# A recurrence in fp32 products, and its two halves with banks, semaphores and tanh of their own

## The reference, cut to what matters

```python
xb = jnp.einsum('bsd,ed->sbe', x, B)

def step(h, xb_t):
    h = jnp.tanh(h @ A.T + xb_t)
    y = h @ C.T
    return (h, y)
```

## Time and profile before

| | us |
|---|---|
| median of 3 runs | 909.51 |
| lowest and highest | 907.95, 910.41 |
| the profiled execution | 910.45 |
| its span, first to last instruction | 908.6 |
| the recurrence in it, from the first tanh to the first product with C | 36.40 to 83.57 |

### The profile page before, as it was taken

How to read it: one execution, slowest core, us unless ns; L and a number is a source line. 1 busy time by engine, 2 the same in 40 slices (tenths; PEclk the granted TensorE clock), 3 DMA queues, 4 the chain that set the end, 5 groups by cost and what they waited for, 6 DMA issues and landing times.

```text
span 908.6 us, 13681 instructions
## 1 busy us (share of the span) xinstructions
PE 785.4 (86%) x4875; PEld 599.0 (66%) x4954; DVE 349.3 (38%) x1002; ACT 250.1 (28%) x583; POOL 133.2 (15%) x100
## 2 busy tenths in 40 slices
PE   8878779999972668897896989999998988999997
PEld 5466439988541334564574558999984555999995
DVE  1434650000319996545765742111114551111113
ACT  1222114433243340436166122212220021122221
POOL 1000020000204991012204030000004012000004
PEclk9855889999995999799997979999999979999998
DMA  9500056995132532000000044999954024799972
GB/s 338 219 3 2 1 223 223 323 306 196 32 107 61 152 99 105 1 0 1 0 1 0 1 161 151 321 319 321 323 208 156 0 71 191 231 327 320 320 235 84
DMA packets 39590, 139.27 MB, mean 153 GB/s; under 512 B 5744, under 2 KB 20288, under 8 KB 27904
## 3 DMA queue, kind: packets, MB, share of 16 engines
q1 hardware_dynamic: 37312, 132.88, 43.4%
q0 software_dynamic: 2240, 5.90, 1.9%
HBM read 127.40 MB, written 11.35 MB: 153 GB/s over the span
## 4 chain that ended last, share of the span: by engine, by line
PE 66%; DVE 14%; DMA 5%; issue 5%; ACT 5%; POOL 3%; DVEq 0%; POOLq 0%; SPq 0%; ACTq 0%
PE PS L428 63%; DVE arena L1616 4%; POOL arena L1216 2%; DMA arena<-x_slots 1%; DVE stats L1297 1%; PE PS L485 1%; PE PS L451 1%; POOL arena L1229 1%; DMA arena<-y_slots,posu 1%; DMA arena<-w_moe 1%; ACT arena L1012 1%; DMA x_slots<-XH,posu 1%; ACT XT L911 1%; DMA y_slots<-arena 1%; DMA arena<-bc_scratch 0%
## 5 line engine op out<-in xcount | busy, mean ns | idle before, releaser
L428 PE MATMUL PS<-arena 128*128 128x128 f32 (+4 forms) x3348 | 421.6, 280 | 28.1 <-ACT arena L1012 9.8
L428 PEld LDWEIGHTS PS<-arena 128*128 128x128 f32 (+2 forms) x3348 | 368.7, 172 | 69.5 <-issue 18.3
L428 PE MATMUL PS<-warm 128*128 128x512 bf16 (+1 forms) x397 | 106.4, 379 | 14.8 <-DVE rs L1281 9.0
L1441 DVE TENSOR_TENSOR arena<-arena,PS 128x384 f32<-128x384 f32 (+1 forms) x62 | 30.3, 488 | 199.2 <-ACT arena L949 199.2
L428 PEld LDWEIGHTS PS<-warm 128*128 128x128 bf16 x476 | 46.4, 100 | 66.9 <-DVE rs L1281 12.9
L1216 POOL DMA_INDIRECT arena<-y_slots,posu x25 | 23.9, 954 | 384.6 <-DMA y_slots<-arena 377.9
L949 ACT ACTIVATE arena<-PS 128x384 f32<-128x384 f32 x62 | 30.4, 490 | 162.2 <-PE PS L428 162.2
L428 PE MATMUL PS<-arena,ident 128*128 128x512 f32 (+1 forms) x128 | 39.6, 456 | 38.1 <-POOL arena L1229 38.1
L1229 POOL TENSOR_TENSOR arena<-arena 128x1152 f32<-128x1152 f32 x16 | 56.1, 3509 | 48.8 <-DVE arena L1616 48.4
L1453 DVE SCALAR_TENSOR_TENSOR H<-arena,wgt,H 128x256 f32<-128x256 f32 (+1 forms) x25 | 11.9, 477 | 124.8 <-DMA arena<-y_slots,posu 124.4
L428 PEld LDWEIGHTS PS<-arena,ident 128*128 128x128 f32 x128 | 21.2, 196 | 56.6 <-POOL arena L1229 40.1
(11 more groups left out here) (253 smaller groups left out, 756.1 us busy)
## 6 DMA issues: line engine op xcount, KB each, us to landing
arena<-w_moe SPq DMA_DIRECT2D x31, 1152.0 KB, 5.7
arena<-w_moe SPq DMA_DIRECT2D x31, 1024.0 KB, 5.2
arena<-w_moe SPq DMA_DIRECT2D x24, 1026.0 KB, 6.6
arena<-bc_scratch SPq DMA_DIRECT2D x32, 288.0 KB, 3.8
arena<-x_slots SPq DMA_DIRECT2D x43, 128.0 KB, 2.2
y_slots<-arena SPq DMA_DIRECT2D x43, 128.0 KB, 5.0
wsh<-w_sh SPq DMA_DIRECT2D x1, 2176.0 KB, 8.3
wl_s<-w_l SPq DMA_DIRECT2D x1, 2048.0 KB
```

The lines of the kernel that those rows point to most:

```text
L428: return nc.tensor.matmul(out_, l, r, start=start, stop=stop, skip_group_check=True)
L1441: ins = v.tensor_tensor(hid_b[x][:, 0:full], sg_s[x][:, 0:full], PS[:, 2 * x + 1, 0:full], ALU.mult)
```

## The change

The three bf16 terms go, of A and of h, with the four splitting instructions of VectorE and its three in every step. A step is now four fp32 products, each a block of the fp32 matrix A (`wrnn_s[:, 0]`) with 16 columns of `HN`, read where tanh wrote them. The two halves of the output have a semaphore each: `rnn_z0` is signalled when half 0 of the sum is complete, `rnn_z1` when half 1 is, and ScalarE does tanh on each half as soon as it is there, one instruction of 16 columns in place of two with 32. TensorE waits for `rnn_h0` before the products that read half 0 of h, and for `rnn_h1` before those that read half 1. Odd and even steps have the four products in different orders.

```diff
--- before.py
+++ after.py
@@ -221,12 +221,6 @@
 
         HN = part(PATCH_K * (T + D), KD, T)
 
-        o_ = PATCH_K * (T + D) + KD * T
-        A_p = part(o_, 3 * KD * D // 2).bitcast(BF16).rearrange("p (i k d) -> p i k d", i=3, k=KD)
-        A_rest = part(o_ + 3 * KD * D // 2, KD, D)
-        h_p = part(o_ + 5 * KD * D // 2, 3 * KD * NB // 2).bitcast(BF16).rearrange("p (i k b l) -> p i k b l", i=3, k=KD, l=1)
-        h_rest = part(o_ + 5 * KD * D // 2 + 3 * KD * NB // 2, KD, NB)
-
         U1 = KD * T
         xs, zs, dr, dl, dx, ys = (part(i * U1, KD, T) for i in range(6))
         dA = [PS[:, 3 + 2 * d:5 + 2 * d, :].rearrange("p b c -> p (b c)")[:, 0:T] for d in range(KD)]
@@ -628,22 +622,28 @@
             last.then_inc(sem("rnn_x"), 1)
             HNv = HN[:, :, :].rearrange("p k (b l) -> p k b l", l=L)
 
-            def rnn_step(lh, at, t):
-
-                for i, (what, parts_of_a) in enumerate((("rnn_h1", 3), ("rnn_h2", 2), ("rnn_h3", 1))):
-                    pe.wait_ge(sem(what), t)
-
-                    for a_ in range(parts_of_a):
-                        for m in range(KD):
-                            for k in range(KD):
-                                last = mm(PS[:, 4 + 2 * lh + m, at:at + NB], A_p[:, a_, k, 128 * m:128 * (m + 1)],
-                                          h_p[:, i, k, :, 0], False, False)
-                return last
-
-            pe.wait_ge(sem("A_split"), 1)
+            def rnn_step(t):
+
+                def product(m, k):
+                    z = PS[:, 4 + 2 * (t % 2) + m, NB * (t // 2):NB * (t // 2 + 1)]
+                    return mm(z, wrnn_s[:, 0, k, 128 * m:128 * (m + 1)], HNv[:, k, :, t - 1], False, False)
+
+                pe.wait_ge(sem("rnn_h0"), t)
+                product(0, 0)
+                if t % 2:
+                    pe.wait_ge(sem("rnn_h1"), t)
+                    product(0, 1).then_inc(sem("rnn_z0"), 1)
+                    product(1, 0)
+                else:
+                    product(1, 0)
+                    pe.wait_ge(sem("rnn_h1"), t)
+                    product(0, 1).then_inc(sem("rnn_z0"), 1)
+                product(1, 1).then_inc(sem("rnn_z1"), 1)
+
             for t in range(1, L):
-                rnn_step(t % 2, NB * (t // 2), t).then_inc(sem("rnn_z"), 1)
-            pe.wait_ge(sem("rnn_h"), L)
+                rnn_step(t)
+            for m in range(KD):
+                pe.wait_ge(sem(f"rnn_h{m}"), L)
             token_products("attn0", lambda k, j: HN[:, k, tsl(j)], KD, lambda k: wrnn_s[:, 2, k, :])
 
 
@@ -1004,13 +1004,12 @@
 
             HNv = HN[:, :, :].rearrange("p k (b l) -> p k b l", l=L)
             act.wait_ge(sem("rnn_x"), 1)
-            nc.scalar.activation(h_p[:, 0], PS[:, 4:6, 0:NB], ACT.Tanh).then_inc(sem("rnn_h1"), 1)
-            nc.scalar.activation(HNv[:, :, :, 0:1], PS[:, 4:6, 0:NB], ACT.Tanh).then_inc(sem("rnn_h"), 1)
-            for t in range(1, L):
-                z = PS[:, 4 + 2 * (t % 2):6 + 2 * (t % 2), NB * (t // 2):NB * (t // 2 + 1)]
-                act.wait_ge(sem("rnn_z"), t)
-                nc.scalar.activation(h_p[:, 0], z, ACT.Tanh).then_inc(sem("rnn_h1"), 1)
-                nc.scalar.activation(HNv[:, :, :, t:t + 1], z, ACT.Tanh).then_inc(sem("rnn_h"), 1)
+            for t in range(L):
+                for m in range(KD):
+                    if t:
+                        act.wait_ge(sem(f"rnn_z{m}"), t)
+                    z = PS[:, 4 + 2 * (t % 2) + m, NB * (t // 2):NB * (t // 2 + 1)]
+                    nc.scalar.activation(HNv[:, m, :, t], z, ACT.Tanh).then_inc(sem(f"rnn_h{m}"), 1)
 
 
             act.wait_ge(sem("lru_reduced"), 1)
@@ -1493,23 +1492,6 @@
                 all_stats(H)
 
 
-            dve.wait_ge(sem("ld_rnn"), 32)
-            link(v.tensor_copy(A_p[:, 0], wrnn_s[:, 0]))
-            link(v.tensor_tensor(A_rest[:, :, :], wrnn_s[:, 0], A_p[:, 0], ALU.subtract))
-            link(v.tensor_copy(A_p[:, 1], A_rest[:, :, :]))
-            v.tensor_tensor(A_p[:, 2], A_rest[:, :, :], A_p[:, 1], ALU.subtract).then_inc(sem("A_split"), 1)
-
-            HNv = HN[:, :, :].rearrange("p k (b l) -> p k b l", l=L)
-            for t in range(L - 1):
-                dve.wait_ge(sem("rnn_h"), t + 1)
-                v.tensor_tensor(h_p[:, 1], HNv[:, :, :, t:t + 1], h_p[:, 0], ALU.subtract).then_inc(sem("rnn_h2"), 1)
-                v.tensor_tensor(h_rest[:, :, :, None], HNv[:, :, :, t:t + 1], h_p[:, 0], ALU.subtract)\
-                    .then_inc(sem("rnn_rest"), 1)
-                dve.wait_ge(sem("rnn_h2"), t + 1)
-                dve.wait_ge(sem("rnn_rest"), t + 1)
-                v.tensor_tensor(h_p[:, 2], h_rest[:, :, :, None], h_p[:, 1], ALU.subtract).then_inc(sem("rnn_h3"), 1)
-
-
             dve.wait_ge(sem("lru_b"), 1)
             c_ = lambda i: lru_c[:, i:i + 1]
             link(v.tensor_scalar(c_(5), c_(2), float(np.pi / 2), None, ALU.add))
```

## The result

| | before | changed |
|---|---|---|
| median of four runs, us | 908.73 | 921.25 |
| lowest and highest, us | 904.72, 910.41 | 919.58, 923.50 |
| the profiled execution, us | 910.45 | 923.50 |
| its span, us | 908.6 | 921.6 |
| first tanh to the first product with C, us | 47.17 | 58.89 |

The ratio of the changed kernel to the one before is 1.0143, with a 95% interval from 1.0113 to 1.0174: 13 us slower, between 10 and 16. The forecast was 923.3, in a range of 916 to 930. One number further down needs a word here: three of the ten executions of e5 ran at a mean clock of 0.90 where the others had 0.94 to 0.95, took 955 to 971 us, and are not in its ratio.

What follows compares the result with a forecast made beforehand. TensorE's weight loads were to bound the recurrence at 1.765 us a step against 1.337 for the three-engine loop; the change costs 13.8 us, taking the profiled 910.45 to 924.3, forecast as 923.3, range 916 to 930.

Steps and rivals of the forecast that it cites:

- The bound: Recurrence: TensorE's own loads replace the three-engine loop as the bound, 1.765 us a step against 1.337.
- A load costs 0.213 us at 1.2 GHz, the columns nothing: Recurrence products: weight loads start 0.213 us apart at the lower clock, and 16 strided columns add nothing to that pace.
- Rival 2: Recurrence: a load costs 107 ns at either clock, so 1.19 us a step and 904.5 us; chance 0.01.
- rival 3: Recurrence: strided columns stand behind each load, 0.266 us per load, 2.13 us a step, 935 us; chance 0.05.
- The clock: Recurrence: TensorE runs at 1.2 GHz after about 38.84 us, as before, with 2.1 steps run until then.
- The way back and the waits: Recurrence: half a result is back 0.76 us after its last load starts; one 0.12 us wait per pair of steps.
- The stage: First tanh to the products with C: these start at 97.4 us instead of 83.57, costing 13.8 us.
- What follows: From the products with C on: the same work later, also beginning at the lower clock, with no cost added.
- VectorE's early start: VectorE's preparation for a later sublayer and first additions to H can run early, but gain nothing.

Runs made afterwards that it cites:

- e5: The changed kernel with three bf16 matmuls of 512 columns added behind every step; ratio 0.9999 to the kernel before.
- e3: The changed kernel with 64 in place of 128 stationary columns in each product of the recurrence; 898.51 us, ratio 0.9874 to the kernel before.
- e6: The kernel before with its bf16 terms, each half of the channels given its own semaphore, tanh and splitting instructions; ratio 1.0014.
- e10: The changed kernel itself run again beside the kernel before on the same chip; 925.41 us, ratio 1.0143.
- e7: The kernel before with two bf16 matmuls of 512 columns added per step; ratio 0.9945.
- e9: The kernel before with two bf16 matmuls of 512 columns added per step, run once more; ratio 0.9951.

## Why the prediction was right

- **The bound.** Right: TensorE's loads stand in a row in place of the way round three engines. VectorE has nothing to do in the window (0.00 us busy).
- **A load costs 0.213 us at 1.2 GHz, the columns nothing.** Right, shown by e3 (0.107 for half the width) and by 0.213 from start to start in the stretch (0.216 with the waits). Rival 2 (107 ns at either clock) and rival 3 (columns behind the load) fall.
- **The clock.** Right, and the step on which the sign hung. The first steps show the other side, 1.02 us each at 1.00 where I had 1.035, and so does e5. The clock fell later than I had it, 3.4 us after the first tanh (at 40.64) where before it was 2.4 (at 38.84). So more steps ran fast, about 3.2 for 2.1: 1.1 steps x 0.7 = 0.8 us of the stage. In the nine profiles that lose the clock in the stage it falls 2.1 to 3.6 us after the first tanh, so this term is good to about 1 us.
- **The way back and the waits.** The term was a little too large: 0.48 us from the last load to the tanh where I had 0.51, as the stride adds nothing beyond its columns (matmuls of 376 ns, 14 more than for 8 columns). After a wait the second load follows 0.165 us behind the first and not 0.213. Against that stands a second wait, of 0.05 us for half 1, which I had at nothing. So two steps are 3.46 us where I had 3.53, and 32 steps save 1.1 us.
- **The stage.** By the sum 13.8 us longer; measured 11.7. The two points above are 1.9 of the 2.1 us of difference.
- **What follows.** I let it begin "the same work later". The products with C take 7.7 us where they took 6.2:

```profile
95.75 0.20 ACT L1012 ACTIVATE arena<-PS 128x16 f32<-128x16 f32 x1 [0.66 <-PE PS L422]
...
96.09 7.66 PE L422 MATMUL PS<-wrnn_s,arena 128*128 128x256 f32 x20 [0.38 <-ACT arena L1012]
...
99.89 0.69 DVE L1482 TENSOR_TENSOR TMP<-PS,XH 128x512 f32<-128x512 f32 x1 [69.30 <-PE PS L422]
...
102.78 0.69 DVE L1482 TENSOR_TENSOR TMP<-PS,XH 128x512 f32<-128x512 f32 x1 [2.20 <-PE PS L422]
```

The clock was back at 102.08, 6.0 us after their start, and before at 86.62, 3.05 us after. That is 1.4 us that my sum had only in its range, and it makes up for most of what the stage fell short: 11.7 + 1.4 = 13.1 us, where the ratio says 13 and the sum said 13.8. That it comes out so near is luck in part. The 1.4 us is no price of the change: e6, with the bf16 steps, has 7.7 us too, and e10 has 7.0; in the nine profiles the clock comes back 3.0 to 6.0 us after the start of these products. In the same two profiles the first tanh came 0.8 us later in the changed kernel and what stands behind the products with C was 1.0 us shorter, and two executions of one kernel can differ by far more there (the last section).
- **VectorE's early start** brought nothing, as said: DVE waits from its additions until 99.89 for TensorE.

## What to carry to other kernels

A chain of small products, each needing the last, is priced by the weight load and by the clock it will run at, so look for a row of the same operand type and clock in your own trace before taking fewer instructions for less time: 4 fp32 products here cost TensorE more than 24 bf16 ones. Splitting a dependent step into halves pays what the other half's work covers: 16.5 us beside fp32 products of 0.43 us each, nothing beside four bf16 matmuls of 0.1 us together. And a busy TensorE can still be at half its clock; where its waits leave gaps, columns of idle matmuls in them can bring it back for nothing, but try how many, and look at every execution.

## What the runs showed of the hardware that I had not expected

- Full engine, half clock: PE busy 55.0 of 55.3 us at 0.50. With two added matmuls of 512 columns a step the clock fell as well (PE busy 98%), with three it stayed up (100%), in seven executions of ten as their times and mean clocks say.
- The first load after a wait is followed by the next after 0.165 us, at 0.50, and not after 0.213. The records of the loads overlap, so TensorE's waits of 0.05 and 0.09 us are seen only in the starts.
- VectorE's instructions of 16 columns, 0.17 to 0.18 us each, start 0.09 to 0.10 us apart when nothing orders them.
- e7 and e9 are the same kernel; their recurrence ends at 83.7 and 83.8 us, and what follows takes 830.5 us in one profile and 816.2 in the other. So one pair of spans says little about a change of 13 us here; the stage's own time does.
